# One query product for two heads, and the turn of the context moved into the next strip

## What is computed

```python
h = relu(layernorm(x))
q, k, v = (h @ W.T + b for W, b in ((Wq, bq), (Wk, bk), (Wv, bv)))       # split into 4 heads of 64
scores = einsum('bhnd,bhjcd->bhnjc', q, kc) / sqrt(64)
scores = where(mask == 0, -10, clip(scores, -10, 10))
attn = softmax(scores, axis=-1)                                         # within each chunk of 256 keys
ctx = einsum('bhnjc,bhjcd->bhnd', attn, vc)                             # summed over the chunks
out = layernorm(ctx @ Wo.T + bo + h) * gamma + beta
x = x + out
```

## Time and profile before

| | |
|---|---|
| median of 3 runs | 5316.2 us (5311.72 to 5316.87) |
| the profiled execution | 5312.18 us, its span 5310.4 us |
| granted TensorE clock | 0.976 of full speed on average |
| PE busy | 4904.6 us (92%) |
| PE weight loads | 4439.3 us (84%) |
| DVE busy | 3759.9 us (71%) |
| ACT busy | 2901.6 us (55%) |
| POOL busy | 1333.0 us (25%) |

### The profile page before, as it was taken

The page is one execution under the profiler, slowest core; times in us unless marked ns, Lnnn a source line. Parts: engine busy times, 40 slices in busy tenths (PEclk is TensorE's granted clock), DMA queues, the critical chain, the costliest instruction groups (busy, mean ns, idle before and its releaser), DMA issues. The chain is left out here.

```text
span 5310.4 us, 139580 instructions
## 1 busy us (share of the span) xinstructions
PE 4904.6 (92%) x56608; PEld 4439.3 (84%) x56608; DVE 3759.9 (71%) x7147; ACT 2901.6 (55%) x3112; POOL 1333.0 (25%) x1472
## 2 busy tenths in 40 slices
PE   2999999999999999999999999975988988989889
PEld 2889888898899889988989889964988978879889
DVE  3666666666666666666666666655888888888888
ACT  2444444444444444444444444434877877778788
POOL 1243334333243324333434333330000000000000
PEclk7999999999999999999999999997999999999999
DMA  5000000000000000000000000003021121120211
GB/s 192 1 17 9 13 9 17 13 9 9 9 21 9 9 13 17 9 13 9 17 13 9 9 9 13 5 27 118 25 74 60 38 67 53 43 73 25 74 52 35
DMA packets 100028, 164.41 MB, mean 31 GB/s; under 512 B 5088, under 2 KB 91488, under 8 KB 92960
## 3 DMA queue, kind: packets, MB, share of 16 engines
q1 hardware_dynamic: 98464, 144.80, 8.4%
q0 software_dynamic: 896, 10.23, 0.5%
HBM read 112.79 MB, written 38.03 MB: 28 GB/s over the span
## 5 line engine op out<-in xcount | busy, mean ns | idle before, releaser
L573 PEld LDWEIGHTS outs<-v_s,probs 128*128 128x128 f32 x16384 | 1973.6, 192 | 81.5 <-issue 3.3
L573 PE MATMUL outs<-v_s,probs 128*128 128x128 f32 x16384 | 1983.9, 275 | 0.6 <-DVE probs L788 0.6
L661 ACT ACTIVATE slot<-slot,shift 128x1024 f32<-128x1024 f32 x1024 | 1111.4, 1088 | 1429.7 <-PE slot L563 1429.7
L788 DVE SCALAR_TENSOR_TENSOR probs<-slot,bound 128x1024 f32<-128x1024 f32 x1024 | 1250.7, 1224 | 721.8 <-ACT slot L661 709.3
L1346 ACT ACTIVATE cond<-s_all,d_sign 128x1024 bf16<-128x1024 f32 x1024 | 1132.2, 1143 | 281.5 <-DVE u L1507 276.0
L421 POOL TENSOR_TENSOR ctx_sum<-ctx_sum,ctx_part 128x256 f32<-128x256 f32 x896 | 647.8, 729 | 1248.3 <-DVE ctx_part L804 1247.5
L562 PE MATMUL slot<-q_hi,k_hl 128*128 128x512 f32 x2048 | 902.2, 441 | 1.1 <-DVE q_lo L744 1.1
L1507 DVE TENSOR_TENSOR u<-cond,mask 128x1024 f16<-128x1024 bf16 x1024 | 691.3, 683 | 169.5 <-ACT cond L1346 109.0
L1236 PE MATMUL sums<-x_plain,u 128*128 128x65 f16 x16384 | 619.3, 195 | 203.9 <-DVE u L1515 158.9
L1241 PE MATMUL sums<-x_mixed,u 128*128 128x130 f16 x8192 | 801.7, 221 | 4.7 <-issue 4.6
L563 PE MATMUL slot<-q_lo,k_hl 128*128 128x512 f32 x2048 | 801.9, 392 | 0.0
(11 more groups left out here) (130 smaller groups left out, 3829.3 us busy)
## 6 DMA issues: line engine op xcount, KB each, us to landing
s_all<-s_turned SPq DMA_DIRECT2D x32, 1024.0 KB, 4.9
adj_in<-in_adj SPq DMA_DIRECT2D x16, 1024.0 KB, 5.8
xs<-in_x SPq DMA_DIRECT2D x32, 512.0 KB, 4.8
x<-y SPq DMA_DIRECT2D x32, 512.0 KB, 3.3
x_s<-x SPq DMA_DIRECT2D x32, 512.0 KB, 5.9
o_s<-x SPq DMA_DIRECT2D x16, 1024.0 KB, 5.4
out<-o_s SPq DMA_DIRECT2D x16, 1024.0 KB, 5.0
mask_t<-mask SPq DMA_DIRECT2D x1, 4096.0 KB, 11.1
```

The lines of the kernel that those rows point to most:

```text
L573: end = nc.tensor.matmul(outs[i % OUTS][:, q, :], probs[:, i % PROBS, r, q * P:(q + 1) * P], v_s[:, c * JC + r, h * E1:h * E1 + P], start= ...
L661: nc.scalar.activation(slot[:, :, :], slot[:, :, :], ACT.Exp, bias=shift[:, 0:1], scale=SCALE).then_inc(act_done, 1)
L788: nc.vector.scalar_tensor_tensor(probs[:, i % PROBS, :, :], spot(kind, "step", s, i)[:, :, :], P_LOW, bound[:, (i // H) % 2, :, :], ALU.ma ...
```

## The change

- `wq_s` holds Wq once, as it is. A query product (`queries`) gives 64 rows for each of two heads: two matmuls of 128 x 512 in place of four. The eviction writes each head's 64 rows to both halves of the partitions, so ACT and DVE do four instructions of 64 partitions per product in place of two of 128. On DVE the second product's two heads are evicted one after the values of step 30 and one after those of step 31.
- At the end of a strip the products stand behind the scores of step 31 and behind the next values, not behind the strip's last values. At the end of a batch the first two keys stand there, and the queries stand behind values 3 and 5.
- The turn comes at step 2 (`TURN_AT`) of the next strip, the projection at step 4, close and statistics two steps later than before (3 and 6), and so do the transpositions and the normalizing of later strips (16 to 23 become 18 to 25, and so on).
- `make_bound(s, 1)` is made inside the strip; the bounds wait accordingly.

Cut to its core:

```diff
-W_AT = 2
+TURN_AT = 2
+W_AT = 4
 BACK = LAG + 1
-T_AT = (24, 27)
-T_LAST_AT = (8, 11)
-TURN_AFTER = 3
+T_AT = (26, 29)
+T_LAST_AT = (10, 13)
+Q_AFTER_V = (3, 5)
...
-        wq_s = sb("wq_s", [P, KC, H, 2, D])
+        wq_s = sb("wq_s", [P, KC, F])
...
-        consts = [(wk_s[:, :, :], wk_t.rearrange("(c p) o -> p c o", p=P)),
+        consts = [(wq_s[:, :, :], wq_t.rearrange("(c p) o -> p c o", p=P)),
+                  (wk_s[:, :, :], wk_t.rearrange("(c p) o -> p c o", p=P)),
...
-            for c in range(KC):
-                consts.append((wq_s[:, c, :, half, :],
-                               wq_t[c * P:(c + 1) * P, :].rearrange("p (h d) -> p h d", h=H)))
...
             def queries(strip, qu, use, slot):
 
                 fill(use)
-                for r in range(2):
-                    for c in range(KC):
-                        last = nc.tensor.matmul(slot[:, r, :], wq_s[:, c, 2 * qu + r, :, :],
-                                                h_t[:, c, strip * STRIP:(strip + 1) * STRIP],
-                                                start=(c == 0), stop=(c == KC - 1))
+                for c in range(KC):
+                    last = nc.tensor.matmul(slot[:, 0, :], wq_s[:, c, qu * P:(qu + 1) * P],
+                                            h_t[:, c, strip * STRIP:(strip + 1) * STRIP],
+                                            start=(c == 0), stop=(c == KC - 1))
                 last.then_inc(slot_filled, 1)
...
                 for s in range(NS):
+                    has_before = s > 0 or not first
                     for i in range(STEPS + LAG):
...
+                        if i == TURN_AT and has_before:
+                            turn(b * NS + s - 1, used(b, kind, "turn", s), spot(kind, "turn", s))
+                        if i == W_AT and has_before:
+                            project(used(b, kind, "turn", s), used(b, kind, "project", s), spot(kind, "project", s))
                         if i < STEPS:
                             scores(s, i)
...
+                        if STEPS - 1 <= i < STEPS - 1 + Q_USES:
+                            qu = i - (STEPS - 1)
+                            if s < NS - 1:
+                                queries(s + 1, qu, used(b, kind, "q", s + 1, qu), spot(kind, "q", s + 1, qu))
+                            elif not last:
+                                keys(0, qu, used(b, kind, "t", 0, 1), used(b, kind, "k", 0, qu), spot(kind, "k", 0, qu))
                         if i >= LAG:
                             values(s, i - LAG)
...
-                    if s < NS - 1:
-                        queries(s + 1, 0, used(b, kind, "q", s + 1, 0), spot(kind, "q", s + 1, 0))
-                        turn(b * NS + s, used(b, kind, "turn", s), spot(kind, "turn", s))
-                        queries(s + 1, 1, used(b, kind, "q", s + 1, 1), spot(kind, "q", s + 1, 1))
...
                 for r in range(2):
                     h = 2 * qu + r
-                    last = nc.scalar.activation(q_hi[:, h, :], slot[:, r, :], ACT.Identity, bias=bq_s[:, h:h + 1])
+                    own = slice(r * D, (r + 1) * D)
+                    for half in (own, slice((1 - r) * D, (2 - r) * D)):
+                        last = nc.scalar.activation(q_hi[half, h, :], slot[own, 0, :], ACT.Identity, bias=bq_s[own, h:h + 1])
...
+            def query_head(qu, r, slot, ends):
+                h = 2 * qu + r
+                own = slice(r * D, (r + 1) * D)
+                for half in (own, slice((1 - r) * D, (2 - r) * D)):
+                    last = nc.vector.scalar_tensor_tensor(q_lo[half, h, :], slot[own, 0, :],
+                                                          bq_s[own, h:h + 1], q_hi[own, h, :].bitcast(F32),
                                                           ALU.add, ALU.subtract)
...
-                        if has_before and i == 1:
+                        if has_before and i == TURN_AT - 1:
+                            copy_turned(used(b, kind, "turn", s), spot(kind, "turn", s))
+                        if has_before and i == W_AT - 1:
                             close(*before, used(b, kind, "project", s), spot(kind, "project", s))
-                        if has_before and i == 4:
+                        if has_before and i == W_AT + 2:
                             close_statistics(*before, used(b, kind, "project", s))
...
+                        if STEPS <= i < STEPS + Q_USES:
+                            qu = i - STEPS
+                            if s < NS - 1:
+                                dve.wait_ge(act_done, acted(b, s, i))
+                                query_head(qu, 0, spot(kind, "q", s + 1, qu), False)
+                                if qu == 0:
+                                    query_head(qu, 1, spot(kind, "q", s + 1, qu), True)
...
+                        if i == STEPS + BACK - 1 and s < NS - 1:
+                            query_head(Q_USES - 1, 1, spot(kind, "q", s + 1, Q_USES - 1), True)
```

More of the change, by code:

```diff
@@ L177, in count_uses @@
         for i in range(STEPS):
+            if i == TURN_AT:
+                use("turn", s)
             if i == W_AT:
@@ L183, in count_uses @@
         if s < NS - 1:
-            use("q", s + 1, 0)
-            use("turn", s)
-            use("q", s + 1, 1)
+            for qu in range(Q_USES):
+                use("q", s + 1, qu)
     if last:
-        use("turn", NS - 1)
+        use("turn", NS)
         use("project", NS)
         return place
-    for n, (s, hp) in enumerate(k_order()):
-        if n == TURN_AFTER:
-            use("turn", NS - 1)
+    for s, hp in k_order():
         use("k", s, hp)
@@ L196, in count_uses @@
         use("v", k)
-    for qu in range(Q_USES):
-        use("q", 0, qu)
+        if k in Q_AFTER_V:
+            use("q", 0, Q_AFTER_V.index(k))
     return place
@@ L304, in used @@
             place = USES[kind][name]
-            skipped = 0 if kind == FIRST and place < USES[kind][("project", 0)] else 1
+            skipped = 2
+            if kind == FIRST:
+                skipped = sum(place >= USES[kind][(gone, 0)] for gone in ("turn", "project"))
             return b * BATCH_USES + PROLOGUE_USES - skipped + place
@@ L322, in acted @@
             return PROLOGUE_ACTS + b * BATCH_ACTS + s * STRIP_ACTS + i + 1
[L324 to L326 removed]
+        last_turn = used(B - 1, LAST, "turn", NS)
+        consts = [(wq_s[:, :, :], wq_t.rearrange("(c p) o -> p c o", p=P)),
+                  (wk_s[:, :, :], wk_t.rearrange("(c p) o -> p c o", p=P)),
                   (wv_s[:, :, :], wv_t.rearrange("(c p) o -> p c o", p=P)),
@@ L452, in batch @@
                         add(b, s, i)
-                        if s == 0 and not first and i in (19, 22):
-                            pair = (i - 19) // 3
+                        if s == 0 and not first and i in (21, 24):
+                            pair = (i - 21) // 3
                             pool.wait_ge(norm_res_done, 2 * (b - 1) + pair + 1)
                             residual(b * T_USES + T_USES - 1 + pair, hs[:, (NS - 1) * IT + 2 * pair:(NS - 1) * IT + 2 * pair + 2, :])
-                        if s == 0 and not last and i == 21:
+                        if s == 0 and not last and i == 23:
                             inverse_std(b * NS + 2, tiles(NS - 1))
                         if s > 0 and not last:
-                            if i == 15:
+                            if i == 17:
                                 inverse_std(b * NS + s + 2, tiles(s - 1))
@@ L663, in batch @@
                         c, h = divmod(i, H)
-                        if h == 1 and 2 <= c + 1 < NC:
-                            make_bound(s, c + 1, used(b, kind, "step", s, c * H - 1))
+                        if h == 1 and c + 1 < NC:
+                            make_bound(s, c + 1, clipped(b, kind, s, c))
                     if s < NS - 1:
-                        queries(0, used(b, kind, "q", s + 1, 0), spot(kind, "q", s + 1, 0))
                         make_bound(s + 1, 0, used(b, kind, "step", s, STEPS - H - 1))
-                        queries(1, used(b, kind, "q", s + 1, 1), spot(kind, "q", s + 1, 1))
-                        make_bound(s + 1, 1, used(b, kind, "step", s, STEPS - 1))
+                        for qu in range(Q_USES):
+                            queries(qu, used(b, kind, "q", s + 1, qu), spot(kind, "q", s + 1, qu))
                 if not last:
+                    make_bound(0, 0, used(b, kind, "step", NS - 1, STEPS - H - 1))
                     for s, hp in k_order():
@@ L674, in batch @@
                     for qu in range(Q_USES):
-                        make_bound(0, qu, used(b, kind, "step", NS - 1, STEPS - H - 1 + qu * H))
                         queries(qu, used(b, kind, "q", 0, qu), spot(kind, "q", 0, qu))
@@ L742, in queries @@
                 for r in range(2):
-                    h = 2 * qu + r
-                    last = nc.vector.scalar_tensor_tensor(q_lo[:, h, :], slot[:, r, :],
```

(12 more changed lines are left out.)

82 lines of the change are left out of this document (37 added, 45 removed).

## The result

| | before | after |
|---|---|---|
| median of 4 runs each | 5313.96 us (5310.36 to 5316.87) | 5363.44 us (5361.4 to 5365.6) |
| profiled execution, its span | 5312.18 us, 5310.4 us | 5361.4 us, 5359.6 us |
| granted TensorE clock, mean | 0.976 | 0.969 |
| start of the second layer (its first load on POOL, `mask` from `mask_t`) | 3577.2 us | 3614.3 us |
| from there to the end of the span | 1733.2 us | 1745.3 us |

The changed kernel is slower: the ratio is 1.0093, with a 95% interval of 1.0076 to 1.0111. That is 49.5 us by the medians and 49.2 us by the spans of the profiled executions. Of these, **37.1 us** (3614.3 - 3577.2) arise in the first layer and **12.1 us** (1745.3 - 1733.2) in the second, whose code is the same. The forecast was +19, all of it in the first layer.

The account below looks back on a forecast made before the run. First layer bound by PE; -110.1 of work, +31 and +32 at boundaries, +4.3 and -2.3 at the start, +64 for the adds gave +19 us, so 5335 us; range 5288 to 5352.

Parts of the forecast that it names:

- work of PE: Query products in the first layer: 1.72 us each instead of 3.44, two at each of 32 strips, -110.1 us.
- 24 inner boundaries: Strip boundaries inside a batch: the turn waits 1.95 us for q1's slot, scores(2) 0.35 for a clip; +1.3 each, +31 us.
- 7 batch boundaries: Between batches: second query product and scores(0) wait 2.6 us each, scores(2) 0.75; +4.5 each, +32 us.
- start: Before the first batch: scores directly behind both query products cost +4.3 us; three fewer constant loads give -2.3 us.
- adds hold `scale(8)`: Strips with a predecessor: scale(8) on VectorE waits for POOL's add behind its closing chain, PE stands 2.15 us; +64 us.
- decisive step: Projection and statistics two steps later: POOL's late add holds VectorE 4.3 us and PE 2.15 us, 31 times; +64 us.
- first rival: Claimed that POOL's adds don't stop PE behind the later projection: 5271 us, faster; chance 0.12.
- the side "faster": Whole kernel: outcome below 5305.6 us, given a chance of 0.26 in all.
- The eviction's length: Query product's four 64-partition instructions, priced by the key row without overlap: 2.8 us on ScalarE, 3.0 on VectorE.
- the overlap rivals: Query evictions overlap: on both engines 5300 us, faster, chance 0.13; on ScalarE alone 5319, no change, chance 0.10.
- the one with a dearer crossing: Query evictions that cross halves cost ScalarE more, mattering from a mean of 0.82 us; at 1.1, 5414 us; chance 0.05.

Follow-up runs that it names:

- chain_between_adds: The change, with POOL's closing chain cut up: two instructions ahead of the adds, the other five one behind each add of steps 4 to 8; 5291.13 us, ratio 0.9957.
- second_layer_shifted: The change, with 195 PE instructions that only count a semaphore put at the start of the second layer; 5351.98 us, ratio 1.007.
- Both opposite edits: The change with POOL's chain cut up between the adds, 5291.13 us; the kernel before with only the output's statistics two steps later, 5382.12 us.

## Why the prediction was right and wrong

| term, us | forecast | measured | from |
|---|---|---|---|
| work of PE | -110.1 | -110.1 | 1.72 a product, 64 products |
| 24 inner boundaries | +31 | +27 | period 100.0 to 97.7 in chain_between_adds: 3.44 saved, 1.1 given back |
| 7 batch boundaries | +32 | +24 | period 129.2 to 130.9 there, 1.7 of it a drop: 3.44 saved, 3.4 given back |
| start | +4.3 - 2.3 | +1 | queries start 1.7 earlier, stand 2.4 more |
| adds hold `scale(8)` | +64 | +63.5 | after against chain_between_adds |
| clock behind stands | none | +32.5 | 19 drops |
| second layer | none | +12.1 | second_layer_shifted |
| sum | +19 | +50 | +49.2 measured |

**The decisive step was right in place, mechanism and size.** The wait of VectorE was 4.15 us where 4.3 were forecast, 31 times; PE's behind it 1.75 (54.1 / 31), and with the step's later start 2.05 a strip (63.5 / 31) where 2.15 - 3 / 31 were. Both opposite edits show it. The first rival (5271) and with it a good part of the side "faster" fell with this.

**The eviction's length was right.** Two key instructions were the right row to take: four `q_hi` took 2.75 us and four `q_lo` 3.04, forecast 2.8 and 3.0. By the spacing on VectorE the Trainium skill's rule ("VectorE: DVE Perf Modes", section "Two Vector instructions with no wait between them") agrees: 0.76 us each (3.04 / 4), no overlap. The Trainium skill's figure in "ScalarE: Activation LUTs", section "What ACT_TABLE_LOAD costs", by which back-to-back activations overlap by about 93 ns, does not hold here: 2.75 us for four whose mean is 0.68 us leaves no overlap. So the overlap rivals fell (5300 and 5319), and so did the one with a dearer crossing (5414), whose 0.82 us was not reached.

**The two boundary terms were a little too large,** 12 us together. At inner boundaries the turn waited 1.8 us for the forecast 1.95, and scores(2) 0.2 for 0.35. At batch boundaries scores(2) waited 0.88 where 0.75 were forecast, but only at the one boundary where no drop follows the stand of scores(0). At the other six the drop stretches scores(0), scores(1) and the turn, and the clip is done by then; second_layer_shifted has four boundaries without that drop, and there scores(2) wait 0.86 to 0.88.

**The step that failed is the first one:** "So the first layer is bound by PE, and what counts is the PE work removed and each wait that makes PE stand." Each wait was priced by its own length, and the half clock that can follow a stand was put at nothing, without a reason. In before, PE stands at most 1.1 us at a time in the strips, and no drop of the clock follows; so none of the rows that the prediction used priced a longer stand. The change makes 70 stands of 1.3 to 4.2 us in the first layer (31 + 24 + 8 + 7 in the list of waits), and 18 of them were followed at once by a half clock: ten of the 14 at batch boundaries, four of the 31 behind `scale`, three of the 24 of the turn, one at the start (the nineteenth drop is behind the last strip's turn, which waits 1.53 us for POOL). The 19 drops cost 32.5 us, two thirds of the result. The price stood in the trace of before, in the second layer: PE stands there 22 times for 2.3 us, and ten times the half clock follows at once. One of the ten, the stand and then its window:

```profile
3835.19 1.84 PE L1236 MATMUL sums<-x_plain,u 128*128 128x65 f16 x32 [2.29 <-DVE u L1515]
```

```profile
3836.00:3838.00 2.00, 2.00 (x33) 2.00 (x31) 1.99 (x4) 1.63 (x2) 0.00 (x0) 0.50 0.04 8
```

That was reason for a term with a wide range, from nothing to 1.7 us for each new stand of about 2 us.

**The second sentence that failed** is "The second layer (from about 3573 us) is not touched." Its code wasn't; its place in PE's program was, and that made 12.1 us. Without these two, the terms that the forecast had come to +5 where it said +19, and that would have measured as no difference. So the direction was right, but partly by luck: the adds' term took back the gain of the shorter product, as forecast, and what made the kernel measurably slower was the clock and the shift. The range ended at 5352 and did not hold 5363.

## What to carry to other kernels

When PE-bound work is cut and waits like these (1.7 us and more) take its place, price the wait twice: its length, and the half clock that may follow it; look through the whole trace, also its other stages, for stands as long as those that the change makes, and see what the clock does behind them. When a step is moved later, look at the in-order engine that serves it (here POOL): if a long chain stands ahead of short instructions that others wait for, cut the chain up between them first, which here turned +49 us into -22. And compare the unchanged parts of a program by their length too: here 195 instructions fewer ahead of an unchanged loop made it 12 us longer, which no reading of the changed part will explain.

## What the runs showed of the hardware that wasn't expected

- The granted clock fell from 2.4 to 1.2 GHz amid a stretch in which PE was 96% busy (3166.66 of 3300 us), right behind stands of 1.8 to 4.2 us, 18 of the 70 stands that the change makes; not once behind the 31 stands of 0.96 us of before, but behind ten of the 22 stands of 2.3 us in before's second layer. A drop took up to 1.71 us. Which of the like stands is followed by one the runs don't tell: inside a batch it is one in eight, at batch boundaries ten of 14.
- PE stands about 6 to 8 us at the head of a pass of the second layer's loop, with nothing shown that it waits for. With 195 instructions ahead of the layer that only count, the sum of such stands went from 56.0 to 49.3 us, and the layer from 1745.3 to 1733.4 us.
- Activations of 64 partitions that read one half of PSUM and write alternately to both halves of SBUF cost 0.68 us each with no overlap, the same as keys that stay in their half.
